# Adding beta to ten of the batches by accumulating transfers begun by GpSimd instead of GpSimd additions

## The reference

```python
def layer_norm(x, gamma, beta, eps=1e-5):
    mean = jnp.mean(x, axis=(-2, -1), keepdims=True)
    var = jnp.mean(jnp.square(x - mean), axis=(-2, -1), keepdims=True)
    return (x - mean) * jax.lax.rsqrt(var + eps) * gamma + beta

out = silu(scale * layer_norm(x, gamma, beta) + shift) @ W_in + b_in
out = silu(scale * layer_norm(out, gamma, beta) + shift) @ W_out + b_out
return out + x
```

## Time and profile before

| | us |
|---|---|
| median of two runs | 82.7 (82.47 and 82.94) |
| span of the profiled execution, first to last instruction | 80.7 |
| median less span | 2.0 |
| PE busy | 75.0 (93% of the span) |
| DVE busy | 61.3 (76%) |
| ACT busy | 55.8 (69%) |
| POOL busy | 53.3 (66%) |

### The profile page before, as it was taken

The page is one execution under the profiler, slowest core; times in us unless marked ns, Lnnn a source line. Parts: engine busy times, 40 slices in busy tenths (PEclk is TensorE's granted clock), DMA queues, the critical chain, the costliest instruction groups (busy, mean ns, idle before and its releaser), DMA issues.

```text
span 80.7 us, 1314 instructions
## 1 busy us (share of the span) xinstructions
PE 75.0 (93%) x293; PEld 37.2 (46%) x293; DVE 61.3 (76%) x181; ACT 55.8 (69%) x174; POOL 53.3 (66%) x63
## 2 busy tenths in 40 slices
PE   4999899999989999999999899999999899999950
PEld 1367547468633444444453443444454344445420
DVE  1085797879899979999879868886194697989560
ACT  4202410999939998977999997799936998967000
POOL 4000283999999999999999999999999303020000
PEclk9999999999999999999999999999999999999999
DMA  1799999999500000201130033030307200030835
GB/s 8 279 446 398 426 384 400 406 410 404 238 8 4 0 0 0 103 27 64 70 127 3 0 130 132 6 134 0 130 4 282 108 0 0 0 129 1 325 141 184
DMA packets 4903, 11.92 MB, mean 148 GB/s; under 512 B 672, under 2 KB 928, under 8 KB 4768
## 3 DMA queue, kind: packets, MB, share of 16 engines
q1 hardware_dynamic: 4752, 11.33, 36.7%
q10 hardware_dynamic: 144, 0.52, 1.6%
HBM read 7.65 MB, written 4.19 MB: 147 GB/s over the span
## 4 chain that ended last, share of the span: by engine, by line
POOL 41%; PE 27%; issue 25%; DVE 2%; POOLq 0%; ACT 0%; ACTq 0%
POOL act L326 16%; POOL act L331 11%; PE acc L978 11%; POOL act L320 7%; PE acc L849 6%; POOL rstd L304 5%; PE acc L954 5%; PE acc L989 2%; POOL rstd L314 1%; PE acc L852 1%; PE acc L999 1%; DVE o_sb L716 1%; PE stat_m L1007 1%; PE stat L898 0%; DVE spread L621 0%
## 5 line engine op out<-in xcount | busy, mean ns | idle before, releaser
L426 ACT ACTIVATE act<-act,cond 128x256 f32<-128x256 f32 x64 | 35.9, 594 | 5.6 <-POOL act L331 3.6
L978 PE MATMUL acc<-act,wout_sb 128*128 128x512 f32 x60 | 27.5, 600 | 0.0
L954 PE MATMUL acc<-act,win_sb 128*128 128x512 f32 x56 | 26.9, 608 | 0.5 <-ACT act L426 0.2
L331 POOL TENSOR_TENSOR act<-act,beta_sb 128x512 f32<-128x512 f32 x13 | 16.5, 1281 | 0.7
L326 POOL TENSOR_TENSOR act<-act,gamma_sb 128x512 f32<-128x512 f32 x13 | 16.6, 1284 | 0.3
L978 PEld LDWEIGHTS acc<-act,wout_sb 128*128 128x128 f32 x60 | 10.9, 189 | 12.4 <-issue 9.0
L446 ACT ACTIVATE squares<-acc,shift 128x256 bf16<-128x256 f32 x32 | 14.7, 464 | 2.1 <-PE acc L954 1.3
L704 DVE SCALAR_TENSOR_TENSOR act<-acc,shift,gamma_sb 128x256 f32<-128x256 f32 x32 | 14.3, 476 | 1.4 <-ACT squares L446 1.3
L954 PEld LDWEIGHTS acc<-act,win_sb 128*128 128x128 f32 x56 | 9.8, 190 | 10.5 <-issue 7.5
L711 DVE SCALAR_TENSOR_TENSOR act<-act,rstd,beta_ps 128x512 f32<-128x512 f32 x16 | 11.6, 742 | 3.4 <-issue 2.5
L716 DVE SCALAR_TENSOR_TENSOR o_sb<-acc,const_sb,x_sb 128x512 f32<-128x512 f32 (+1 forms) x17 | 11.9, 713 | 2.4 <-PE acc L978 2.3
(11 more groups left out here) (74 smaller groups left out, 53.7 us busy)
## 6 DMA issues: line engine op xcount, KB each, us to landing
out_dram<-o_sb SPq DMA_DIRECT2D x15, 256.0 KB, 2.0
x_sb<-x_dram SPq DMA_DIRECT2D x7, 512.0 KB, 12.8
w_sb<-w_dram SPq DMA_DIRECT2D x1, 1024.0 KB, 6.2
wss_sb<-wss_dram SPq DMA_DIRECT2D x1, 768.0 KB, 8.5
x_sb<-x_dram ACTq DMA_DIRECT2D x1, 512.0 KB, 3.9
w_sb<-w_dram SPq DMA_DIRECT2D x1, 256.0 KB, 4.1
gamma_sb<-gamma_dram SPq DMA_DIRECT2D x1, 256.0 KB, 6.4
wss_sb<-wss_dram SPq DMA_DIRECT2D x1, 256.0 KB, 8.7
```

Of the source, the lines that this page charges most:

```text
L331: nc.gpsimd.tensor_tensor(act1[:, p, :, b], act1[:, p, :, b], beta_sb[:], ALU.add).then_inc(z1_pool, 1)
L426: return nc.scalar.activation(buf[:, c, b], buf[:, c, b], ACT.Silu, bias=cond[:, 1, c, i:i + 1], scale=cond[:, 0, c, i:i + 1], **kw)
L954: mm = nc.tensor.matmul(y_slot(p, c)[:].rearrange("p b s -> p (b s)"), win_sb[:, k, c * P:(c + 1) * P], act1[:, p, k].rearrange("p b s -> ...
L978: mm = nc.tensor.matmul(bank_of(("O", p, c, 0, BP))[:].rearrange("p b s -> p (b s)"), wout_sb[:, k, c * P:(c + 1) * P], act2[:, p, k].rear ...
```

## The change

In ten of POOL's thirteen batches, both of each of the pairs 3 to 7, the addition of beta is replaced by a transfer from `beta_sb` to the batch in `act1` with an accumulating write (`accum_op=ALU.add`), begun from POOL's queue at the place where the addition stood. It waits for the same two things. Each of the ten has a semaphore of its own, raised by 16 when it has landed, and ACT's first activation of such a batch waits for that instead of for `z1_pool`. The three batches (0, 1), (1, 1) and (2, 1) keep their addition on POOL, and DVE's batches are as they were.

```diff
-Z1_POOL = ((0, 1), (1, 1), (2, 1), (3, 0), (3, 1), (4, 0), (4, 1), (5, 1), (5, 0), (6, 0), (6, 1), (7, 0), (7, 1))
+Z1_POOL = ((0, 1), (1, 1), (2, 1))
+Z1_SENT = ((3, 0), (3, 1), (4, 0), (4, 1), (5, 1), (5, 0), (6, 0), (6, 1), (7, 0), (7, 1))
...
+        z1_sent = {(p, b): sem(f"z1_sent{p}_{b}") for p, b in Z1_SENT}
...
+            def send_beta(p, b):
+                pool.wait_ge(beta_in, 16)
+                pool.wait_ge(scaled_pool, count(SCALED_POOL, (p, b)))
+                pool.dma_start(act1[:, p, :, b], beta_sb[:], accum_op=ALU.add).then_inc(z1_sent[p, b], 16)
...
             weigh_gamma(3, 1)
             weigh_gamma(3, 0)
-            weigh_beta(3, 0)
-            weigh_beta(3, 1)
+            send_beta(3, 0)
+            send_beta(3, 1)
             layer1_rstd(4)
             layer2_rstd(1)
...
             weigh_gamma(5, 1)
             centre1(5, 0)
-            weigh_beta(5, 1)
+            send_beta(5, 1)
             weigh_gamma(5, 0)
-            weigh_beta(5, 0)
+            send_beta(5, 0)
             layer1_rstd(5)
             layer2_rstd(3)
...
             weigh_gamma(6, 1)
-            weigh_beta(6, 0)
-            weigh_beta(6, 1)
+            send_beta(6, 0)
+            send_beta(6, 1)
             weigh_gamma(7, 0)
             centre1(7, 1)
-            weigh_beta(7, 0)
+            send_beta(7, 0)
             weigh_gamma(7, 1)
-            weigh_beta(7, 1)
+            send_beta(7, 1)
             layer2_rstd(5)
...
                 elif (p, b, c, 1) in Z1_DVE:
                     act.wait_ge(z1_dve, count(Z1_DVE, (p, b, c, 1)))
+                elif (p, b) in Z1_SENT:
+                    act.wait_ge(z1_sent[p, b], 16)
                 else:
                     act.wait_ge(z1_pool, count(Z1_POOL, (p, b)))
```

More of the change, by code:

```diff
@@ L358, in _ @@
             weigh_gamma(4, 1)
-            weigh_beta(4, 0)
-            weigh_beta(4, 1)
+            send_beta(4, 0)
+            send_beta(4, 1)
             centre1(5, 1)
```

## The result

The changed kernel took 90.38 us (median of two runs, 89.89 and 90.86) against 82.7 us. The measured ratio is 1.096, with an interval of 1.0864 to 1.1056 (the two medians alone give 1.093). The profiled execution is the one of 89.89 us, with a span of 88.1 us against 80.7. So 7.4 us of span are to be found.

What follows compares the result with a forecast made beforehand. PE's packed last 14.4 us, started when POOL's last beta addition let ACT go, was taken as the bound; the last landing's +4.6 us on 82.7 gave 87.3 us, range 83 to 94.

Steps and rivals of the forecast that it cites:

- likeliest case: Transfers land after about 4 us, with POOL held up to 1.4 us per issue: 85 to 90 us, chance 0.52.
- dear issue: Rival: each issue holds POOL 2.0 us and its transfer lands after 4.7 us: 92.6 us, chance 0.23.
- d = 1.28: Time POOL is held by beginning one transfer, taken as 1.28 us, like the addition it replaces.
- freed POOL: Rival: POOL held only 0.33 us per issue, landing after 2.0 us, PE the bound: 82.2 us, chance 0.08.
- L = 4.0: Time from beginning a transfer until ACT may read the batch, taken as 4.0 us.
- short landing rival: Same mechanism with landing after 2.6 us, only the last batch counting, +1.3 us: 84.0 us, chance 0.17.
- Pair 3, ACT +2.7, PE at 35.2: First transfer lands at 33.3, ACT starts 2.7 us late, PE at about 35.2 instead of 33.58.
- Pair 4, PE +2.4: Transfer begun at 37.34 lands at 41.35; PE starts pair 4 at 43.25 instead of 40.87.
- The way back to POOL: PE's lateness delays DVE's variance, moving POOL's power for pairs 6 and 7 from 47.11 to about 48.7, +1.6 us.
- The end set by the last landing: Last transfer begun at 63.1 lands at 67.1, ACT +4.6 us; PE, packed from there, cannot take it back.

Runs made afterwards that it cites:

- c9: Changed kernel with its ten accumulating transfers sent onto finished batches of three pairs earlier, ACT not waiting for them, beta not added: 82.93 us, ratio 1.0052.
- c1: Changed kernel with the ten additions of beta left out altogether, neither added by POOL nor sent: 81.27 us, ratio 0.9846 against the kernel before.
- c8: Changed kernel with POOL's steps reordered so that a centring or product stands between two transfer issues: 89.94 us, ratio 1.0885 against the kernel before.
- c11: Changed kernel with POOL's issues spaced by other steps and ten idle matmuls on PE before pair 6: 89.32 us, ratio 1.085 against the kernel before.
- c10: Changed kernel with plain copies onto finished batches instead of accumulating transfers, ACT waiting for their landing, beta not added: 83.75 us, ratio 1.0107.
- c5: Changed kernel with only the four batches of pairs 6 and 7 sent, pairs 3 to 5 keeping POOL's addition: 86.4 us, ratio 1.0448.
- c7: Changed kernel with ten idle matmuls of zeros on PE ahead of the statistics matmul before pair 6: 88.95 us, ratio 1.0794 against the kernel before.
- c6: Changed kernel with only the six batches of pairs 3 to 5 sent, pairs 6 and 7 keeping POOL's addition: 87.17 us, ratio 1.055.
- c2: Changed kernel with its accumulating transfers sent to a scratch buffer zeroed at the start, ACT not waiting for them: 84.47 us, ratio 1.0259.

## Why the prediction was right and wrong

The time was 90.4 us where I forecast 87.3, slower as forecast and inside the range of 83 to 94, but just above the likeliest case's own 85 to 90. The upper part of the range was there for a dear issue, which did not come; that it also covered late second landings and a fallen clock is luck. Right was that the landing costs and the issue does not; short was the size, by these steps:

- **d = 1.28, POOL wins nothing: right.** The issues add up to 13.0 us, 1.3 each, and POOL's busy time is unchanged. From the start of pair 3's first product with gamma to the first centring of pair 4 POOL took 6.91 us (26.36 to 33.27) against 6.78 before (26.62 to 33.40). c9 puts all ten at 0.4 us of the end. The rival of a dear issue (d = 2.0) and that of a freed POOL both fall; even freed of all work on beta (c1) the gain would be 1.1 us.
- **L = 4.0: right as a median, mis-sized for the batches that count.** The second of two adjacent issues took 4.9, 5.6 and 5.4 us at pairs 3, 4 and 6. I dismissed the DMA engines as mostly empty; they were, before the change, but one accumulating transfer takes 1.81 us of all 16. That the neighbour makes the second late is shown by c8 and c11 (3.8 to 4.0 with distance); that it queues on the engines is argued, with the plain neighbours of c10 for it. The short landing rival (2.6) fits a plain copy, 2.7 in c10, at a price of 1% there. The rule cited for 2.6 us (the Trainium skill, DMA: Bandwidth & Descriptors, section Anatomy of one DMA — SWDGE (gpsimd) path) thus agrees with the plain copies and not with the accumulating ones, 3.7 to 5.6.
- **Pair 3, ACT +2.7, PE at 35.2: the first half right (33.45), PE late by 1.0 more (36.22)**, since the third activation waited for (3, 1) until 35.38.
- **Pair 4, PE +2.4: this is the largest failed term.** PE came +3.9. The 41.35 of the sum is (4, 0), begun at 37.34; it was begun at 37.20 and landed 4.5 us later, at 41.7. But PE's third activation is of (4, 1), begun at 38.31, which landed at 43.94. By the sum's own d and L that would have been 38.62 and 42.62, near enough to its 43.25 for PE; the error is the 5.6 us.
- **The way back to POOL, +1.6 for the power of pairs 6 and 7: nearly right in place, late in size.** POOL waited 1.61 us for DVE's variance and ran it at 50.03, forecast 48.7. The last issue began at 64.59, forecast 63.1.
- **The end set by the last landing, PE packed 14.4 us behind it: wrong for this execution.** Pair 6's second landing held the row sums, PE stood 2.40 us at 63.01, and its products, on a fallen clock, then lasted until (7, 1) was ready. c5 shows the standstill alone. The last batch was not far behind, some 6 us later for PE's last six products, and in c8 it does set the end. My sum put +4.6 on the last landing where the ledger has +3.9 at pair 4 and +1.9 of added idle at pair 6: 4.6 against 5.8, by another way.
- **A missing term: the clock.** The last packed stretch took 1.5 us more because the granted clock fell to 0.53 after the standstill. c9 (6.26) and c7 (6.42 against 7.80 for the same fourteen products) show it; c5's four runs put it at nearer 0.8. Of the 2.7 us of span that the sum lacked (7.3 against 4.6), the clock is 1.5 and the later starts, pair 4's above all, are 1.2.

## What to carry to other kernels

Where a transfer takes the place of an engine's step on a path without slack, compare the step's duration with begin to landing, here 1.28 against 3.7 to 5.6 us; that POOL was held about as long by beginning it as by doing it cost only 0.4 us (c9). Cost each transfer of a group with the landing that it has behind its neighbours (here 4.9 to 5.6 us; the engine time per transfer, 1.8 us from the share of its queue, gives the distance), not at the median of all. And when a late arrival makes PE stand, count the clock after it as well as the gap, and check first what the change could win at most: leaving the step out showed 1.5%.

## What the runs showed that I had not expected

- An accumulating transfer of 256 KB within the on-chip memory took over twice the engine time of a plain one, 1.81 against 0.76 us of all 16, and 3.7 to 5.6 us to land against a median of 2.7 (2.5 to 5.1). Its issue's row is 1.15 to 1.89 us long, a plain one's 0.72 to 0.91.
- GpSimd's row after an issue begins before the issue's row ends and is longer: the power at 31.28 took 1.88 us, against 1.02. From the start of each issue of pair 3 to the next row's start were 0.93 and 0.87 us, so the length of an issue's row (1.37 median) is not what it delays; starts are the better measure.
- An issue right behind GpSimd's own product on the same batch stood 0.55 us; the addition in the same place had 0.7 us of idle time ahead of it for all thirteen together.
- The length of a standstill alone did not tell whether the clock fell. In the changed kernel it stayed full after 2.77 us at pair 3 and fell after 2.40 at pair 6; in c7 and c6 it fell at pair 3 after 2.88 and 2.87, and in c8 it stayed full after 2.20 and 2.19. Why one execution has it and another not stays open.
- A GpSimd memset of 128 x 5120 took 4.4 us at the start of c2. DVE's first row, of 128 x 16, began beside it and took 2.07 us instead of 0.23, ending (5.87) as the memset ended (5.84); the first transfer, 25 us later, still began 1.4 us late.
